# Expert phase of a four-layer transformer kernel: second bias added in the eviction, added rows one turn later in GpSimd's order

## The reference

```python
w_full = zeros((N, 8)).at[arange(N)[:, None], top_i].add(softmax(top_v))
for e in range(8):
    mid = gelu(flat @ exp_W1[e] + exp_b1[e], approximate=False)
    y_e = mid @ exp_W2[e] + exp_b2[e]
    out = out + w_full[:, e:e + 1] * y_e
```

## Time and profile before

| | us |
|---|---|
| median of 3 runs | 3957.21 (3955.8 to 3958.84) |
| the profiled execution | 3943.67 |
| its span, first to last instruction | 3941.9 |
| PE busy | 3356.2 (85%) |
| DVE busy | 2328.6 (59%) |
| ACT busy | 1536.7 (39%) |
| POOL busy | 453.6 (12%) |

### The profile page before, as it was taken

One profiled execution on the slowest core, in us unless ns is written; L12 is line 12 of the kernel. 1 busy time (PEld: TensorE's weight loads), 2 busy tenths in 40 slices (PEclk: granted clock), 3 DMA queues, 4 the chain that ended last, 5 costly groups with the idle time before them and its releaser, 6 DMA issues. The chain is left out here.

```text
span 3941.9 us, 54941 instructions
## 1 busy us (share of the span) xinstructions
PE 3356.2 (85%) x21150; PEld 1812.6 (46%) x21150; DVE 2328.6 (59%) x5238; ACT 1536.7 (39%) x2367; POOL 453.6 (12%) x335
## 2 busy tenths in 40 slices
PE   7887887888888499997889887898888989789988
PEld 5433433433433378886445324453234543344532
DVE  7765664665674456665643575635667246764357
ACT  5354344344335234443542333524234433254232
POOL 0000001001001244442000040000310002200003
PEclk9999899999989799998999999999998999899999
DMA  7302302402311787775111302103121022201130
GB/s 276 84 10 104 83 10 86 101 10 71 108 18 53 173 222 222 215 228 145 23 28 28 71 1 66 28 16 55 29 55 36 3 34 65 55 12 28 28 71 11
DMA packets 197737, 292.19 MB, mean 74 GB/s; under 512 B 88228, under 2 KB 154422, under 8 KB 180344
## 3 DMA queue, kind: packets, MB, share of 16 engines
q1 hardware_dynamic: 180453, 268.10, 25.9%
q0 software_dynamic: 17024, 20.53, 2.6%
HBM read 210.02 MB, written 77.23 MB: 73 GB/s over the span
## 5 line engine op out<-in xcount | busy, mean ns | idle before, releaser
L895 PE MATMUL ps<-ternary_W,ident 128*128 128x512 f16 x2148 | 636.8, 410 | 64.9 <-SPq L546 14.0
L2128 DVE TENSOR_REDUCE max_parts<-ps 128x1 f32<-128x512 f32 (+3 forms) x768 | 383.6, 551 | 159.5 <-PE ps L1016 118.6
L1556 ACT ACTIVATE arena<-ps 128x256 f32<-128x256 f32 (+7 forms) x512 | 318.8, 650 | 406.5 <-PE ps L1036 236.9
L1881 POOL TENSOR_TENSOR arena<-arena 128x640 f32<-128x640 f32 x108 | 175.8, 1628 | 1909.6 <-ACT arena L1797 1909.1
L895 PEld LDWEIGHTS ps<-ternary_W,ident 128*128 128x128 f16 x2148 | 214.1, 104 | 372.4 <-issue 111.2
L2050 DVE CAST arena<-arena 128x256 f16<-128x256 f32 (+2 forms) x424 | 156.1, 368 | 286.9 <-ACT arena L1721 155.6
L1625 ACT ACTIVATE arena<-ps 77x1024 f32<-77x1024 f32 x192 | 190.5, 1017 | 206.1 <-PE ps L1204 203.4
L1721 ACT ACTIVATE arena<-ps,arena 128x256 f32<-128x256 f32 x312 | 148.1, 475 | 259.6 <-PE ps L847 245.6
L2052 DVE TENSOR_TENSOR arena<-arena 128x256 f16<-128x256 f32 (+2 forms) x424 | 236.7, 558 | 14.5
L2583 DVE TENSOR_REDUCE max_parts<-ps 128x1 f32<-128x512 f32 x256 | 165.8, 686 | 122.3 <-PE ps L1413 121.4
L1797 ACT ACTIVATE arena<-ps 128x1024 f32<-128x1024 f32 x128 | 130.7, 1024 | 251.9 <-PE ps L1429 251.8
(11 more groups left out here) (450 smaller groups left out, 7396.6 us busy)
## 6 DMA issues: line engine op xcount, KB each, us to landing
arena<-scr_expert_weights SPq DMA_DIRECT2D x52, 1024.0 KB, 7.4
k_stack<-scr_expert_weights SPq DMA_DIRECT2D x26, 1024.0 KB, 7.5
q_stack<-scr_q SPq DMA_DIRECT2D x108, 128.0 KB, 4.1
scr_q<-arena SPq DMA_DIRECT2D x48, 256.0 KB, 2.5
k_stack<-scr_q SPq DMA_DIRECT2D x72, 128.0 KB, 4.7
butterflied_W_exp<-in_exp_W SPq DMA_DIRECT2D x8, 1024.0 KB, 6.8
butterflied_W_con_turned<-in_exp_W SPq DMA_DIRECT2D x8, 1024.0 KB, 8.8
scr_expert_weights<-q_stack SPq DMA_DIRECT2D x8, 1024.0 KB, 4.0
```

Source lines behind the costliest of these rows:

```text
L895: pe.matmul(s[:, 0:CH], ident[:], Wq1[:, 0, 0:CH], start=True, stop=True)
L1556: act.activation(PR[:, n % NP, kt * P:T], slot(L, "ST", g, kt, j)[:, kt * P:T], ACT.Exp).then_inc(*did("act", L, "exp", g, kt, j))
L1881: pool.tensor_tensor(total, p, total if kt > 1 else q, ALU.add).then_inc(*did("pool", "F3", "PA", h, kt))
L2128: dve.tensor_reduce(mpart[:, j * NT + t, c:c + 1], slot(L, "S", g, t, j, c)[:, 0:n], AX, ALU.max).then_inc(*frees("dve", L, "S", g, t, j, c))
```

## The change

It does two things.

1. The second bias leaves TensorE. The one-hot products, `sel`, its column `row_n` of the constants and the experts' rows in `BR` are gone. Instead SyncE loads the expert's bias row for each tile, broadcast to 128 partitions (128 KB, `b2t[i % 4]`), behind the first bias. ScalarE multiplies it by each token's weight times 64 into `b2w` (a new function `rows_bias`, called after the Gelu of step m = 6: one small and two 128 x 256 operations). VectorE's eviction becomes PSUM times weight plus `b2w`.
2. GpSimd's loop picks tile i and then adds tile i-3, with one turn more.

```diff
@@ SyncE, tile_weights(i)
                 sp.dma_start(b1t[i % 4], A["exp_b1"][bass.ds(e, 1)].rearrange("o p m -> p (o m)")).then_inc(*did(f"ld_b1{i % 4}", i))
+                if i >= 4:
+                    sp.wait_ge(*of("act", "b2w", i - 4, TC4 - 1))
+                sp.dma_start(b2t[i % 4], A["exp_b2"][bass.ds(e, 1)].partition_broadcast(P)).then_inc(*did(f"ld_b2{i % 4}", i))
@@ TensorE, down(i, m)
-                        mm = split3(o, left, parts(w2, m), m == 0 and c % 2 == 0, False, skip_group_check=True)
-                        if m == NM - 1:
-                            chosen_row = sel[:, i:i + 1].to_broadcast([P, P])
-                            pe.matmul(o, chosen_row, BR[:, 0], start=False, stop=False, skip_group_check=True)
-                            mm = pe.matmul(o, chosen_row, BR[:, 1], start=False, stop=True, skip_group_check=True)
+                        mm = split3(o, left, parts(w2, m), m == 0 and c % 2 == 0, m == NM - 1, skip_group_check=True)
@@ ScalarE, experts()
+                def rows_bias(i):
+                    act.wait_ge(*of(f"ld_tab{i % 4}", i))
+                    act.wait_ge(*of(f"ld_b2{i % 4}", i))
+                    if i:
+                        act.wait_ge(*of("act", "b2w", i - 1, TC4 - 1))
+                    act.activation(row_weight[:, i % 2], taken[i % 4][:, :, 1], ACT.Copy, scale=WS).then_inc(*did("act", "weight", i))
+                    act.wait_ge(*of("act", "weight", i))
+                    if i:
+                        act.wait_ge(*of("dve", "y", i - 1, TC4 - 1))
+                    for c in range(TC4):
+                        act.activation(b2w[:, c], b2t[i % 4], ACT.Copy, scale=row_weight[:, i % 2, c:c + 1]).then_inc(*did("act", "b2w", i, c))
...
+                        if m == 6:
+                            rows_bias(i)
@@ GpSimd, the phase's loop
-            for i in range(NTILE + 2):
+            for i in range(NTILE + 3):
                 if i < NTILE:
                     pick_rows(i)
                 if i == 2:
                     pool.memset(VX[0:TC, :, :, DH:QUARTER], 1.0).then_inc(*did("pool", "vx"))
-                if i >= 2:
-                    add_rows(i - 2)
+                if i >= 3:
+                    add_rows(i - 3)
@@ VectorE, tile_tables()
-                tables_step("sel", dve.tensor_scalar(sel[:, 0:NTILE], tile_e, row_n, None, ALU.is_equal))
@@ VectorE, rows_out(i)
-                        dve.tensor_scalar(yt[:, i % 2, c], slot("D", i, c // 2)[:, (c % 2) * D:(c % 2 + 1) * D], taken[i % 4][:, c, 1:2], None,
-                                          ALU.mult).then_inc(*step("y", i, c))
+                        dve.wait_ge(*of("act", "b2w", i, c))
+                        dve.scalar_tensor_tensor(yt[:, i % 2, c], slot("D", i, c // 2)[:, (c % 2) * D:(c % 2 + 1) * D], taken[i % 4][:, c, 1:2], b2w[:, c],
+                                                 ALU.mult, ALU.add).then_inc(*step("y", i, c))
```

More of the change, by code:

```diff
@@ L45 @@
 CTXW = ["A0k", "A0v", "C1k", "C1v", "D2k", "D2v", "E3k", "E3v"]
-BROW = ["B0v", "B0p", "C1o", "D2v", "D2o", "E3v", "F3o", "L2con", "L2down"] + [f"e{e}" for e in range(NE)]
+BROW = ["B0v", "B0p", "C1o", "D2v", "D2o", "E3v", "F3o", "L2con", "L2down"]
 BCOL = ["B0q", "B0k", "D2q", "D2k", "E3q", "E3k", "ln1_g", "ln1_b", "ln2_g", "ln2_b"]
@@ L322, in build @@
         route = VX[:, :, :, :].rearrange("p l h d -> p (l h d)")
-        before_p, idf, tile_n, row_n = route[:, 0:P], route[:, 128:136], route[:, 136:136 + NTILE], route[:, 199:200]
+        before_p, idf, tile_n = route[:, 0:P], route[:, 128:136], route[:, 136:136 + NTILE]
         lgc = route[:, 200:264].rearrange("p (t e) -> p t e", e=NE)
@@ L345, in build @@
         tile_ids = area(62, 2 * NTILE).bitcast(I32)
-        sel = area(62.5, 64, F16)
+        b2t = [area(58 + i, D) for i in range(4)]
+        b2w = area(51, TC4 * D).rearrange("p (c d) -> p c d", c=TC4)
+        row_weight = area(53, 2 * TC4).rearrange("p (n c) -> p n c", n=2)
         taken = [area(63 + 0.0625 * i, 2 * TC4).rearrange("p (c w) -> p c w", w=2) for i in range(4)]
@@ L439, in build @@
                  "ld_stack0", "ld_stack1", "ld_stack2", "st_l2", "ld_l2", "ld_const2", "ld_const3", "ld_m0", "ld_m1", "ld_wexp0", "ld_wexp1", "ld_wexp2", "st_wexp0", "st_wexp1",
-                 "st_xn", "st_s", "st_tab", "ld_tab0", "ld_tab1", "ld_tab2", "ld_tab3", "ld_b10", "ld_b11", "ld_b12", "ld_b13", "ld_pick0", "ld_pick1",
+                 "st_xn", "st_s", "st_tab", "ld_tab0", "ld_tab1", "ld_tab2", "ld_tab3", "ld_b20", "ld_b21", "ld_b22", "ld_b23", "ld_b10", "ld_b11", "ld_b12", "ld_b13", "ld_pick0", "ld_pick1",
                  "st_y", "ld_sel", "st_out"] + [f"{n}{g}" for n in ("ld_s", "ld_r") for g in range(NG)] + [
@@ L2654, in layouts @@
             "E3v": f["L3_xattn_v_b"], "F3o": f["L3_ffn_bo"], "L2con": f["L2_ffn_b_con"], "L2down": f["L2_ffn_down_bias"]}
-    rows.update({f"e{e}": f["L0_ffn_exp_b2"][e] for e in range(NE)})
     cols = {"B0q": f["L0_ffn_bq"], "B0k": f["L0_ffn_bk"], "D2q": f["L2_xattn_bq"], "D2k": f["L2_xattn_bk"], "E3q": f["L3_xattn_q_b"],
@@ L2687, in layouts @@
     route[:, 136:136 + NTILE] = np.arange(NTILE)
-    route[:, 199] = np.arange(P) - BROW.index("e0")
     none = z((ROWS, 2), np.float32)
@@ L2713, in layouts @@
         "exp_W2": f["L0_ffn_exp_W2"].reshape(NE, NM, P, D).transpose(0, 2, 1, 3).reshape(NE, P, -1),
-        "exp_b1": f["L0_ffn_exp_b1"].reshape(NE, NM, P).transpose(0, 2, 1), "c_route": route, "c_none": none,
+        "exp_b2": f["L0_ffn_exp_b2"], "exp_b1": f["L0_ffn_exp_b1"].reshape(NE, NM, P).transpose(0, 2, 1), "c_route": route, "c_none": none,
         "L1_W1": halves_of(f["L1_ffn_W1"].T), "L1_W2": f["L1_ffn_W2"].T.reshape(NM, P, D).transpose(1, 0, 2).reshape(P, -1),
```

## The result

The changed kernel takes 3985.58 us (median of five runs, 3974.65 to 3992.87), the kernel before 3957.21 beside it (five runs, 3955.8 to 3959.98): a ratio of 1.0069, 95% interval 1.0047 to 1.0090. It is slower, by 28.4 us. So the two profiles differ by 49.1 us of span, more than the medians do. Lines have moved: what was L741 (table), L750 (weights), L1849 (pick), L1858 (add) and L1311 (transposes) is now L743, L752, L1864, L1873 and L1316; the load of the second bias is L759.

What follows compares the result with a forecast made beforehand. After the change a closed loop of table load, picks, adds and landing was to bound the expert phase, not TensorE: 1429.7 + 405.8 (32 turns x 12.68) + 25.9 = 1861.4, 28.3 us more; 3957.2 + 28.3 = 3985.5 us, range 3953 to 4007.

Steps and rivals of the forecast that it cites:

- the circle: GpSimd and SyncE, expert phase: adds of i-4 land, table i loads, tile i is picked, adds of i-3 follow; 12.68 us.
- The length of a turn: From one table load's issue to the next: 8.18 us of issuing plus 4.5 from last add to next table, 12.68 us.
- the first rival: Adds land as fast as in a quiet turn, 3.56 us: a turn of 11.74 us, no change; chance 0.2.
- Table 6 at 1429.73: SyncE's load of table 6 stays at its old time, set by the key loads of turn 2, within 2 us.
- The end: From table 38 to TensorE's last product in the expert phase: 25.9 us, including 5.2 for the second pick's landing.
- the sum: Table 6's time, 32 turns and the end: last product at 1861.4 against 1833.1 before, 28.3 us more.
- The waits: Signs in the changed profile: picks wait some 200 us for tables, transposes some 55 for picked rows, adds no more.
- Edits costed at nothing: One-hot products removed (17 us of TensorE), ScalarE's three operations, VectorE's eviction, the bias load's issue, one comparison less: no time effect.
- The cover of ScalarE and VectorE: TensorE's idle 1.76 us per turn hides ScalarE's delay of about 0.5 us and VectorE's eviction difference of 0.1 us.
- the uncovered bound: ScalarE's delay of the last Gelu, if TensorE's idle time did not hide it: at most 0.5 x 39 = 20 us.
- its three turns: Three profiled turns from add's end to next table, 3.56, 3.88 and 5.16 us, from which 4.5 us was taken.

Runs made afterwards that it cites:

- the order alone: The kernel before with only GpSimd's adds moved one tile later (pick i, add i-3), bias still as one-hot products: 3977.05 us, ratio 1.0053.
- the bias alone: The changed kernel with GpSimd's loop as before (pick i, add i-2), so only the second bias moved: 3951.1 us, ratio 0.9985.
- weights first: The kernel before, four table buffers, SyncE issuing the weights of tile i+3 ahead of its table: 3976.62 us, ratio 1.0059.

## Why the prediction was right, and where it was not

The forecast held: slower by 28.4 us against 28.3, through the circle that the prediction described, of table, picks, adds and landing. The agreement to a tenth is luck, since the profile's own phase is 38.7 us longer. By its steps:

- **The circle decides.** Right. The move alone makes it (12.41 us a turn, 212 us of waiting for tables), and eight table buffers undo it (10.92 us).
- **The length of a turn**, 12.68: measured 12.79. Issuing, 8.18 us, took 8.17 in the turn shown (1483.12 - 1474.95) and 8.40 in the mean of the 32 turns. The 4.5 us from the last add to the next table measured 4.35 by median and 4.39 in the mean, with single turns from 3.8 to 5.4. The quiet 3.56 of the first rival was never reached. Right: the landing is 0.1 us shorter and the issuing 0.2 longer than forecast.
- **Table 6 at 1429.73, with 2 us to either side.** Wrong by 6.7 us. Of these, 3.2 lie ahead of the first table; the other 3.5 come between tables 0 and 6 (82.2 us for 78.7), where the order alone took 80.6 and the bias alone 79.2. The prediction had let both wait behind the key loads for free.
- **The end**, 25.9 us from table 38 to the last product: measured 29.2 (1875.05, the end of the last product). The picks, beside weights and bias, took 1856.02 - 1849.22 = 6.8 us instead of 5.2, and transposes to last product 19.0 instead of 17.3. Most of these 1.7 us more is TensorE's clock: it had waited 2.45 us for the picked rows, and over the next 3.8 us its products stood 0.21 us apart, at a granted clock of 0.56 on average (mostly 1.2 GHz, then 2.4). In the kernel before the same stretch ran at 1.00. The end, 3.3 us, the turns, 3.6, and the first tiles, 3.5, make the 10.4 us by which the profiled phase is longer than the sum (38.7 for 28.3).
- **The waits.** Pick for table 224.1 us for "some 200", transposes for picked rows 52.6 for "some 55", adds for VectorE and TensorE nearly none. Right.
- **Edits costed at nothing.** The products saved 17 us of TensorE and bought nothing while the circle decided: right, and shown by the runs with eight tables, where they are worth 16 to 17. The cover of ScalarE and VectorE held: 0.50 us for each of ScalarE's two operations, 477 ns for the eviction, and 1.5 us of TensorE's waits ended by VectorE. Even without TensorE's idle time, in the kernel with eight tables, a tile takes 10.92 us, so the 20 us of the uncovered bound did not show at all.
- **"Before, the adds that a table waits for were issued two turns earlier, so this closed circle ran over two turns and never decided."** Wrong. Picks hardly waited for tables, but the same wait, with what stood behind it on SyncE, set when the weights left, and they left with the next adds and picks. Eight tables gave the kernel before 17 us. The prediction read only who waits for the table, and not what waits behind it. Nor were its three turns typical: over the 32 turns of the kernel before, the next table left 7.4 us after the adds by median (3.6 to 9.3), since their weights mostly left with the adds. For the changed kernel the choice was still right, because there the weights leave 4.2 us ahead of the adds by median.

The Trainium skill (DMA: Bandwidth & Descriptors, section Anatomy of one DMA — SWDGE (gpsimd) path) makes a GpSimd DMA of 128 KB an estimate of 2.3 us, with no term for what runs beside it. The picks come near it where the weights leave 8.0 us ahead of them (2.8 us) and are far from it where they leave 4.3 and 1.5 us ahead (5.2 and 6.3). What decided here was the part that changes with the traffic.

The version that beats both kernels is the bias in the eviction with eight table buffers, in either order of the adds: 3923 us, 0.9907 and 0.9915 of the kernel before.

## What to carry to other kernels

Before moving a step to a later turn, follow its completion to every buffer that it frees, and ask whether a step of the same queue then waits for it: that closes a loop whose length is the sum of issuing and landing, whatever the bound engine does. Four more index tables of 2 KB were worth 62 us in the changed kernel and 17 in the kernel before; the products that the change saved were worth 16 to 17 with eight tables and little with four. Where a wait stands at the head of a queue, look at what stands behind it as well, big loads above all: here the weights left when the table did, and so met the adds and picks.

## What the runs showed of the hardware that I had not expected

- The landing of small indirect transfers depended here on when they leave against large ones, more than on how full the DMA engines are. With the engines 0.77 busy (the kernel before with eight tables, 1452 to 1790 us) picks landed in 2.8 us, 8.0 us behind the weights; at 0.70, 4.3 us behind them, in 5.2. Within the kernel before alone (1440 to 1800 us), the 25 picks that left 2 to 4 us behind the weights' second issue landed in 5.9 us by median, the 20 at 4 to 6 us in 4.8, the 10 at 6 to 8 us in 3.2. The next table followed the end of the adds' issue after 3.95 us where the weights had left 7.4 us ahead of that end, and after 7.96 us where they had left 0.7 us ahead of it.
- A wait of TensorE can cost more than its length. In the kernel before with weights first, TensorE worked at a granted clock of 1.00 (2.4 GHz), then waited 4.45 us for picked rows, and went on at 0.50 (1.2 GHz) for the next 4.6 us. Windows before, after that wait, and later:

```profile
1640.00:1651.80 11.80, 11.80 (x109) 10.40 (x106) 7.92 (x23) 4.78 (x10) 5.18 (x4) 1.00 0.77 230
1656.26:1660.90 4.64, 4.64 (x22) 3.52 (x23) 0.34 (x2) 1.49 (x3) 2.17 (x3) 0.50 0.59 105
1661.00:1670.00 9.00, 9.00 (x84) 8.08 (x83) 5.44 (x15) 2.85 (x6) 0.00 (x0) 1.00 0.20 61
```

  TensorE ran 22 products in those 4.64 us, where 109 in 11.80 would make 43: the wait of 4.45 us cost about 2.3 us more. Three tiles of 17 to 18 us stand among that kernel's 32 turns.
